# A post-norm decoder layer with routed experts: the fourth row transfer behind the third gated product, two weight splits a step sooner, one row normalisation behind the routing, the last expert's third piece in 64 rows

## The reference, cut to what matters

```
def reference(x, ctx_2048, ...):
    # causal self-attention, 16 heads of 128
    x = layernorm(x + attn(x))
    # linear cross-attention: feature map, sum of k v^T over the context, gate
    x = layernorm(x + xattn(x, ctx))
    # feed-forward: every token goes to its best two of eight experts
    logits = h @ router_weight.T + router_bias
    top_vals, top_idx = top_k(logits, 2); top_w = softmax(top_vals)
    gate, up = (h @ gate_up_proj[e] + gate_up_proj_bias[e])[..., ::2], [..., 1::2]
    gate = minimum(gate, 7); up = clip(up, -7, 7)
    act = (up + 1) * gate * sigmoid(1.702 * gate)
    expert_out = act @ down_proj[e] + down_proj_bias[e]
    x = layernorm(x + sum_e scores[t, e] * expert_out[e, t])
```

## Time and profile before

| | us |
|---|---|
| median of 3 runs | 847.2 |
| the 3 runs | 844.22, 847.2, 847.89 |
| the profiled execution, its own time | 845.05 |
| its span, first to last instruction | 843.2 |
| PE busy | 825.5 (98%) |
| DVE busy | 478.2 (57%) |
| ACT busy | 318.3 (38%) |
| POOL busy | 115.2 (14%) |

### The profile page before, as it was taken

One profiled execution on the slowest core, in us unless ns is written; L12 is line 12 of the kernel. 1 busy time (PEld: TensorE's weight loads), 2 busy tenths in 40 slices (PEclk: granted clock), 3 DMA queues, 4 the chain that ended last, 5 costly groups with the idle time before them and its releaser, 6 DMA issues.

```text
span 843.2 us, 12667 instructions
## 1 busy us (share of the span) xinstructions
PE 825.5 (98%) x4903; PEld 728.9 (86%) x4903; DVE 478.2 (57%) x926; ACT 318.3 (38%) x718; POOL 115.2 (14%) x98
## 2 busy tenths in 40 slices
PE   9999999999999999999999999999999999999995
PEld 7989898989999898988899888888877988888884
DVE  4536445373636454494861234455678786767775
ACT  4543324242433323342343222222144365555534
POOL 0000000000000000000100000101122245545561
PEclk9999999999999999999999999999995999999999
DMA  9990734524030003003110011110076666666345
GB/s 316 361 314 7 223 122 148 193 61 148 7 100 7 25 7 126 1 6 137 51 38 0 1 37 38 63 37 26 26 297 217 221 206 203 202 181 172 71 59 187
DMA packets 36287, 97.79 MB, mean 116 GB/s; under 512 B 7001, under 2 KB 9561, under 8 KB 33537
## 3 DMA queue, kind: packets, MB, share of 16 engines
q1 hardware_dynamic: 32464, 88.70, 30.9%
q0 software_dynamic: 3760, 8.26, 4.8%
HBM read 64.11 MB, written 31.92 MB: 114 GB/s over the span
## 4 chain that ended last, share of the span: by engine, by line
PE 85%; DVE 5%; issue 3%; DMA 2%; ACT 2%; POOL 2%; ACTq 0%; POOLq 0%; DVEq 0%
PE bank L321 66%; PE bank L729 3%; PE bank L633 3%; PE bank L763 3%; PE bank L656 2%; PE bank L824 2%; DMA y_acc<-y,meta 2%; PE bank L715 1%; DVE w_gu L1485 1%; PE bank L801 1%; DVE hh L2003 1%; PE bank L1022 1%; POOL y_acc L566 1%; PE bank L1064 1%; ACT prob L1191 1%
## 5 line engine op out<-in xcount | busy, mean ns | idle before, releaser
L321 PE MATMUL bank<-w_kv,cT 128*125 128x512 f32 x576 | 143.5, 400 | 0.0
L321 PE MATMUL bank<-xT,w_qkv 128*128 128x512 f32 (+1 forms) x672 | 137.8, 365 | 0.7 <-ACT qT L1181 0.7
L321 PEld LDWEIGHTS bank<-xT,w_qkv 128*128 128x128 f32 x672 | 122.1, 188 | 15.8 <-ACT qT L1181 1.1
L321 PEld LDWEIGHTS bank<-w_kv,cT 128*125 128x125 f32 x576 | 104.1, 186 | 23.7
L321 PE MATMUL bank<-x_g,w_gu 128*128 128x288 f32 x768 | 109.3, 300 | 2.8 <-DVE x_g L1485 1.1
L321 PEld LDWEIGHTS bank<-x_g,w_gu 128*128 128x128 f32 x768 | 105.0, 191 | 5.0 <-issue 3.2
L519 POOL TENSOR_TENSOR ln_rs<-ln_ve,half 128x1 f32<-128x1 f32 (+2 forms) x16 | 11.2, 704 | 617.7 <-DVE ln_ve L1614 604.5
L321 PE MATMUL bank<-w_o,zT 128*128 128x512 f32 x336 | 78.7, 392 | 0.0
L321 PE MATMUL bank<-w_qkv,xT 128*128 128x256 f32 x588 | 77.3, 287 | 0.0
L321 PEld LDWEIGHTS bank<-w_o,zT 128*128 128x128 f32 x336 | 62.4, 188 | 12.7
L321 PEld LDWEIGHTS bank<-w_qkv,xT 128*128 128x128 f32 x588 | 72.2, 191 | 0.0
(11 more groups left out here) (182 smaller groups left out, 1242.0 us busy)
## 6 DMA issues: line engine op xcount, KB each, us to landing
x_rows<-blank SPq DMA_DIRECT2D x9, 2084.0 KB, 16.4
raw_gu<-in_w_gu_dram SPq DMA_DIRECT2D x8, 2048.0 KB, 7.8
raw_w<-in_w_qkv_dram SPq DMA_DIRECT2D x22, 512.0 KB, 8.5
raw_dn<-in_w_down_dram SPq DMA_DIRECT2D x8, 1024.0 KB, 5.1
raw_c<-in_ctx_t_dram SPq DMA_DIRECT2D x8, 750.0 KB, 4.4
raw_o<-in_w_o_dram SPq DMA_DIRECT2D x8, 512.0 KB, 4.3
xg<-x_rows SPq DMA_DIRECT2D x7, 512.0 KB, 6.0
raw_kv<-in_w_kv_dram SPq DMA_DIRECT2D x2, 1024.0 KB, 6.9
```

Of the source, the lines that this page charges most:

```text
L321: last = nc.tensor.matmul(mm_out, lhs(a, k), rhs(b, k), start=(k == 0 and i == 0), stop=(k == n - 1 and i == 2))
```

## The change

Four things are edited.

- POOL issues `add_stacked(e - 2)` behind the third `gated` of expert e, not behind the first.
- In the loop of expert 1, `gu_high` and `gu_low` of expert 2's parts k = 2, 3 stand before `h_high` and `h_low` of step 3, not behind them. (For all other experts the list there is empty.)
- `x2_norm` is cut in two: for the last tile (6), `x2_shift` stays in place, and `x2_rows` is run behind `choose(6)`. For the others the order stays, with one more wait that has been met by then.
- The third piece of the last expert becomes stacked too: PE 8 matmuls, not 12; ACT and DVE work on 64 rows, with the row numbers and scores of the same 32 tokens in all four groups of 32 partitions. That takes two more small transfers into `meta` on SP's queue, and no memsets of `sel` and `y7`; `in_meta` counts to 96 and `sel_ok` to 9.

```diff
@@ sync
             sp.dma_start(meta[rows:2 * rows, 2], by_expert[p0:p0 + rows, :, D:L]).then_inc(in_meta, 16)
+            for p in (2 * rows, 3 * rows):
+                sp.dma_start(meta[p:p + rows, 2, LAST_E], x_rows_of(LAST_E * ROWS + p0, rows)[:, D:L]).then_inc(in_meta, 16)
@@ gpsimd
                     for q in range(KC):
                         gated(e, q)
-                        if q == 0 and 0 <= e - 2 < STACKED:
+                        if q == 2 and 0 <= e - 2 < STACKED:
                             add_stacked(e - 2)
                 if e == 1:
                     pool.wait_ge(base_out, 16 * (NT + 1))
-                    pool.wait_ge(in_meta, 64)
+                    pool.wait_ge(in_meta, 96)
@@ tensor
-                if k == 2 and e < STACKED:
+                if k == 2 and e != STACKED:
                     down_stacked(w_dn[e % 2], hT[e % 2], y_bank(e, k))
...
-            pe.wait_ge(m["sel_ok"], 11)
+            pe.wait_ge(m["sel_ok"], 9)
@@ scalar
-                h_high(e, KC - 1, hT[e % 2])
                 for k in splits_at(e, KC):
                     gu_high(e + 1, (e + 1) % 2, k)
+                h_high(e, KC - 1, hT[e % 2])
...
-            for k, (p0, rows) in enumerate(PIECES):
+            for k, rows in enumerate(HELD):
                 act.wait_ge(m["dn_mm"], 3 * LAST_E + (k + 1))
@@ vector
-            def x2_norm(n):
+            def x2_rows(n):
                 normalise(1, n, n + 3, row[:, n, 0:D], "row_ok")
+
+            def x2_shift(n):
                 s = n % 2
+                dve.wait_ge(m["rs_ok"], n + 3)
...
+            def x2_norm(n):
+                x2_rows(n)
+                x2_shift(n)
...
             choose(5)
-            x2_norm(6)
+            x2_shift(6)
             assign(5)
             choose(6)
+            x2_rows(6)
             assign(6)
...
                 hidden(e, KC - 1)
-                h_low(e, KC - 1, hT[e % 2])
                 for k in splits_at(e, KC):
                     gu_low(e + 1, (e + 1) % 2, k)
+                h_low(e, KC - 1, hT[e % 2])
...
             def select(k):
-                rows = HELD[k]
+                rows = P
...
             def last_low(k):
-                rows = PIECES[k][1]
+                rows = HELD[k]
...
             for k in range(3):
                 select(k)
-            for rest in (sel[HELD[2]:P, 2, :], y7[HELD[2]:P, 0, 2, :]):
-                nc.vector.memset(bits(rest), 0.0).then_inc(m["sel_ok"], 1)
```

More of the change, by code:

```diff
@@ L351, in decoder_layer @@
         HELD = (P, P, 2 * (CAP - 2 * P))
+        assert 2 * HELD[2] == P
         SUM_BANK = (0, 1, 2, 3, 5, 6, 7)
@@ L1397, in y_evac @@
                 if i == 0:
-                    act.wait_ge(in_meta, 64)
+                    act.wait_ge(in_meta, 96)
                 if i >= 4:
@@ L2064, in _ @@
             dve.wait_ge(in_late, 16 * 3)
-            dve.wait_ge(in_meta, 64)
+            dve.wait_ge(in_meta, 96)
             for k in range(3):
                 select(k)
-            for rest in (sel[HELD[2]:P, 2, :], y7[HELD[2]:P, 0, 2, :]):
-                nc.vector.memset(bits(rest), 0.0).then_inc(m["sel_ok"], 1)
             for k in range(3):
```

## The result

| | before | changed |
|---|---|---|
| median, us (executions) | 846.47 (11) | 841.82 (11) |
| lowest and highest | 843.32, 847.89 | 840.16, 843.80 |
| profiled execution, its own time | 845.05 | 842.99 |
| its span | 843.2 | 841.2 |

The ratio is 0.995, with a 95% interval of 0.9938 to 0.9962: about 4.2 us faster by the ratio, 4.65 by the medians. So the sizes are first read place by place. Two executions of kernels under Experiments, at 1356.12 us (all without part 1) and 1030.33 us (part 3 alone), were disturbed and are left out of the ratios.

What follows compares the result with a forecast made beforehand. PE, busy 98% of the span, was taken to bound the kernel, with its few waits as the gain. Terms 2.6 + 1.0 + 0.35 + 0.9 = 4.85 us off the executions' mean (846.1) or median gave 841.5 us, range 838.5 to 845.0.

Steps and rivals of the forecast that it cites:

- Part 1: Expert loop: POOL's fourth transfer behind the third product removes the excess of the windows above the floor, 2.6 us.
- with some 5 us to spare: Expert loop: fourth transfer lands 3.0 us after its start, some 5 us before the next three transfers' rows come.
- Part 2: Ahead of expert 2: its last weight splits a step sooner remove PE's idle time, 1.0 us.
- Part 3: End of routing: last tile's normalised row behind the choice shortens PE's wait for `chosen`, 0.35 us.
- Part 4: Program end: last third piece in 64 rows saves four down matmuls, so `combine` starts sooner, 0.9 us.
- it fits by 0.35: Program end: first load of `acc` lands at 827.3, 0.35 us before DVE wants it at 827.65.
- Rival A: Expert loop: another wait keeps DVE's chain as late; the 2.6 falls to 0.5, time 843.6; chance 0.15.
- Rival D: Ahead of expert 2: the change doesn't reach PE; the 1.0 is 0, time 842.5; chance 0.10.
- Rival B: Program end: loads hold it, expert 7's last product delayed 1.25 us; 0.05, not 0.9; time 842.3; chance 0.12.
- Rival C: Experts 0 and 1: full clock returns later, about 2.3 us per quarter, + 11.5 us, time 853; chance 0.05.
- a first sum released by a load: Program end: DVE's first sum released by a load, not PE, would make the 4.85 us sum wrong.
- a clock at 0.50 beyond 652: Expert 0's start: clock still at 0.50 beyond 652 would make the 4.85 us sum wrong.

Runs made afterwards that it cites:

- all without part 1: Changed kernel with the fourth row transfer back behind the first gated product: 844.25 us, ratio 0.9982 to the kernel before.
- part 3 alone: Kernel before with only the last tile's normalised row moved behind the choice: 846.35 us, ratio 1.0002.
- parts 1, 2 and 4: Changed kernel without the move of the last tile's normalised row: 840.91 us, ratio 0.9948; run again, 841.18 us, ratio 0.9936.
- combined_best: Changed kernel without the normalised-row move, fourth transfer behind the second product, ACT scaling expert 6's first piece before the last hidden-row cast: 841.17 us, ratio 0.9948.
- stacked_behind_q1: Changed kernel with the fourth row transfer behind the second product, not the third: 841.1 us, ratio 0.995.
- part 4 alone: Kernel before with only the last expert's third piece stacked in 64 rows: 845.78 us, ratio 0.9997.

## Why the prediction came out as it did

The forecast was 841.5 us and the median is 841.8. The sum took off 4.85 us; measured are 4.2 by the ratio and 4.65 by the medians. Its parts fared as follows.

- **Part 1, 2.6:** the windows gave 2.52, with each on the predicted floor; the time of the edit alone says 3.3 by the ratio, 2.5 by the medians. The mechanism was right. One step in it was wrong: the fourth transfer does not land after 3.0 us "with some 5 us to spare", but after 8.8, and its successors wait for it 5.79 us. The error was to carry a landing time over to another moment without asking which transfers fly there; SP's load of 2 MB stood in the same trace. The demand that POOL should have no idle time ended by a landing failed, though the gain didn't depend on it.
- **Part 2, 1.0:** 1.09 in the trace, 1.6 in the time of the edit alone, with the idle time gone entirely.
- **Part 3, 0.35:** no gain in time in two comparisons. The step that failed is "the row's shift (0.46 us from its start to the next) comes off that wait": DVE's first step of `assign(5)` then waits for PE's count, so 0.19 us come off where the clock is still at full, and nothing in the trace of part 3 alone. The 1.21 us ahead of the ranking became 1.23, not 0.75, and that wait follows the moment of the clock's fall.
- **Part 4, 0.9:** PE's work shrank by 0.93, as 68 matmuls in 15.58 us show. Alone it brought nothing that can be seen (0.3 us, up to 1.3 in the interval), and in its trace a load holds the end. The step that failed is "it fits by 0.35", which took over the landing of the last transfers from before. SP's loads followed POOL's last issue by 3.87 us there and by 5.33 in the changed kernel. The first sum was expected four us or more ahead of 828.57, released by PE; it came 2.81 ahead, released by a load.
- **Rival A** (another wait takes part 1 over) is refuted by the five windows. **Rival D** is refuted by the row at 685.85.
- **Rival B** (the loads hold the end) is what the profiled execution of the changed kernel shows, though not by the cause given. Expert 7's last product wasn't delayed by 1.25 us: it starts at 809.58, 2.98 behind the down product, where it had been 3.22. The transfers took longer to land. The 0.35 us of room can't be far off: in the first trace of parts 1, 2 and 4 SP's loads come 0.31 us later behind the down product's start than in the kernel before (15.18 for 14.87), and PE still releases the sum. Of the seven traces with parts 1 and 4, only the changed kernel's has its first sum released by a load; how many of its executions pay is not known.
- **Rival C** (slower, clock later) didn't occur: the clock was back by 653, well within expert 0's first quarter, at a cost of 0.2 us to this execution and 0.7 at most in others. The rival's price per quarter was too low: 6.01 us at 0.50 from end to end (combined_best), against 3.3 at full clock, is 2.7, not 2.3.

The prediction named a first sum released by a load as a sign that its sum would be wrong, and that sign came. So did, by a little, the sign of a clock at 0.50 beyond 652 (mean 0.80 within 652 to 653). The traces account for the pair: 2.52 + 1.09 + 0.93, less the 0.42 us by which the changed kernel's trace ran late ahead of expert 2, is the 4.12 us by which `combine` came sooner. The load at the end and what follows it then took 2.1 us back. The total is near partly by luck. Parts 1 and 2 measured above their terms (0.7 and 0.6 us by the ratios, both within their intervals), and parts 3 and 4 below (by 0.55 and 0.6). The sum of single measurements, 3.3 + 1.6 - 0.2 + 0.3, is 5.0 us, and each of them is uncertain by about 1 us.

## What to carry to other kernels

Cut the loop into windows and take the shortest as the floor: the excess of the others was the price of the stall to 0.1 us. A wait on a queue should stand behind everything that others need from that engine, even if the waiting transfer then takes three times as long. Before crediting an edit on a path, ask for the next releaser there. At the end, 0.9 us of PE work brought nothing that can be seen alone, and reached the first sum in the traces once the row transfers had been moved ahead. In the routing, 0.46 us of DVE work became 0.19, because DVE then waited for PE. A shorter wait in one trace does not yet speak for the edit: look for the same wait in traces without it.

## What the runs showed of the hardware

- An indirect adding transfer of 64 rows by 512 lands after 3.0 us where its row on POOL has ended before a 2 MB load is issued (kernel before). It takes 8.7 to 9.0 us where the load is issued 1.5 us behind its start and the row ends 0.65 to 0.67 us behind that (changed kernel, experts 2 to 5), and 4.8 and 6.1 us where the row ends 0.05 and 0.30 us behind (stacked_behind_q1).
- A POOL product (0.90 us) and a DVE split (2.29 us) that begin within a microsecond: the loser is not fixed. Where the split started 0.17 or 0.20 us behind the start of POOL's preceding transfer, the product took 2.2; where 0.36, 0.65 or 0.73 behind, the split took 3.99, 3.71 and 3.62. Five traces show this order; none shows why.
- In a stage where PE pauses, the granted clock falls at a moment that moves from execution to execution (within 629 to 630 in six of the fourteen traces, within 632 to 633 in one), and comes back within 650 to 654. PE's next wait for DVE goes with it: 0.54 or 0.55 us in those six, 0.84 to 1.23 where the clock fell within 630 to 632, 1.41 in the last, with and without the edit meant to shorten it. The first 24 gate matmuls so took 4.80 to 6.02 us.
- The wait that a profile puts down to an engine can be a load's: the first sum of part 4 alone, by its distance from `combine`.
